# Last mixture of experts: blocks of 64 slots taken two at a time, activations as the stationary operand, a ring of eight weight buffers

## The chip, the cores and the metric

The kernel runs on one core of one Trainium2 chip. The metric is the device time of one launch in microseconds. The engines that matter here are TensorE (PE in the rows, with PEld for its weight loads), VectorE (DVE), ScalarE (ACT), GpSimd (POOL) and SyncE (SP), which issues the transfers. The kernel writes semaphores and waits by hand; nothing reorders its instructions.

## What is computed

Two layers run over 512 tokens of width 256, each of them attention, a second attention or memory part, and a feed-forward part. The change touches only the last part, the feed-forward part of the second layer: a mixture of eight experts in which each token goes to one.

```python
gate_scores = softmax(einsum('btd,de->bte', x, Wg) + bg)
top1_idx = argmax(gate_scores); top1_weight = gate_scores[top1_idx]
h = silu(einsum('btd,edh->bteh', x, W1) + b1)      # 256 -> 1024, 8 experts
o = einsum('bteh,ehd->bted', h, W2) + b2           # 1024 -> 256
y = sum(o * top1_mask) * top1_weight
x = x + y
```

## The kernel before

`program` runs `xattn0`, `memory0`, `ffn0`, `xattn1` and then `attn1_ffn1`, in which the class `Routed` is the last mixture. `Routed.prepare_sync` (L1985) and `prepare_gpsimd` run inside the attention layer `attn1`, so their loads and constants go beside that layer's work; `Routed.run` (L2016) is a block of its own, which all engines enter together.

P is 128, TT = 4 token tiles, DC = 2 halves of the width, E = 8 experts, NF = 8 pieces of the hidden width F = 1024. The tokens are sorted into blocks of 128 slots, each with one expert. Which expert has how many tokens is known only at run time, so the program always has NB = E + EXTRA = 8 + 3 = 11 blocks: block k below 8 is expert k's first block, and each of the three extra ones belongs to the expert that has overflowed, or to none. The number of an extra block's expert is computed by DVE (`expert`, semaphore `expert_ready`), read by SP into a register (`value_load`), and used in the address of its transfers.

For each block PE does three things, and for each two blocks a fourth:
- `gather(g)` (L2229): 16 products in fp32r with a 0/1 matrix `perm` that pick the tokens of two blocks into `gather_bank`, which DVE copies to `xg` (L2157);
- `hidden(k)` (L2243): 16 fp32 products, a 128x128 piece of `w1` stationary, the block's 128 columns of `xg` moving; the hidden values come out transposed, the hidden index on the partitions. ACT reads them from PSUM, adds the bias `b1` (one value for each partition) and applies Silu in one instruction, eight to a block (L2104), into `h`;
- `output(k)` (L2255): 8 fp32 products, a 128x128 piece of `h` stationary, 256 columns of `w2` moving, into `y_bank`. ACT casts the result to the high part `y_hi` (L2110), DVE forms the rest `y_lo` (L2188);
- `scatter(k)` (L2264): 8 products in fp32r of `permT` (made by DVE, L2162) with the two parts, added up in the banks 5 and 6.

The order on PE is hidden(k), for even k gather(k/2+1), output(k-1), scatter(k-2). The weights of a block are `w1` and `w2`, 1 MB each. Six pairs of buffers form a ring (RING = 6). `prepare_sync` fills all six; SP refills a buffer once `hidden` (for `w1`) or `output` (for `w2`) of the block that used it is done (`reload`, L2056). An fp32 product shows as two matmul records in the trace; an fp32r or bf16 product and a transpose show as one.

Of the kernel before, what the change touches and what calls it, by code (L numbers as in the profile page):

```python
# [19 lines left out]
E = 8  # L20
# [1920 lines left out]
class Routed:  # L1941
# [3 lines left out]
    RING = 6  # L1945

    def __init__(self, core, ctx, tag, weights, norm, out_d):
# [4 lines left out]
        self.EXTRA = (NT - 1) // P  # L1952
        self.NB = E + self.EXTRA
        self.NG = (self.NB + 1) // 2
        sb = lambda name, shape, dt=F32: core.sb(tag + name, shape, dt, ctx)
        self.w1 = [sb(f"_w1_{i}", [P, DC, self.F]) for i in range(self.RING)]
        self.w2 = [sb(f"_w2_{i}", [P, self.NF, D]) for i in range(self.RING)]
        self.b1, self.b2 = sb("_b1", [P, E, self.NF]), sb("_b2", [E, D])
        self.b1x = sb("_b1x", [P, self.EXTRA, self.NF])
        self.rw, self.rb = sb("_gate_w", [P, DC, E]), sb("_gate_b", [P, E])  # L1960
        self.slots = sb("_slots", [P, 2 * P * self.NG])
        self.rows = sb("_rows", [P, self.NB])
# [8 lines left out]
        self.w2_in = [sem(f"w2_{i}_in") for i in range(self.RING)]  # L1971

# [11 lines left out]

    def prepare_sync(self, sp):  # L1985
        sp.dma_start(self.rw[:], self.rw_d.rearrange("(c p) e -> p c e", p=P)).then_inc(self.gate_in, 16)
        sp.dma_start(self.rb[:], self.rb_d.partition_broadcast(P)).then_inc(self.gate_in, 16)
        sp.dma_start(self.b1[:], self.b1_d.rearrange("p (e f) -> p e f", e=E)).then_inc(self.b_in, 16)
        sp.dma_start(self.b2[:], self.b2_d).then_inc(self.b_in, 16)
        for k in range(self.RING):  # L1990
            self.load_w1(sp, k, k)
            self.load_w2(sp, k, k)
# [3 lines left out]
    def prepare_gpsimd(self, pool):  # L1996
# [5 lines left out]
        g.iota(self.rows[:], [[P, self.NB]], base=0, channel_multiplier=1, **exact).then_inc(self.const, 1)  # L2002
        g.iota(self.order[:], [[1, E]], base=-E, channel_multiplier=0, **exact).then_inc(self.const, 1)
        g.iota(self.first[:], [[-P, E]], base=(E - 1) * P, channel_multiplier=0, **exact).then_inc(self.const, 1)
        g.iota(self.steps[:], [[P, self.EXTRA]], base=P, channel_multiplier=0, **exact).then_inc(self.const, 1)
# [10 lines left out]
    def run(self):  # L2016
        core, nc, norm, tag = self.c, self.c.nc, self.norm, self.tag
        x, xn, xnT = core.x, core.xn, core.xnT
        NB, NG, NF, RING, EXTRA = self.NB, self.NG, self.NF, self.RING, self.EXTRA
        with ExitStack() as ctx:  # L2020
            sb = lambda name, shape, dt=F32: core.sb(tag + name, shape, dt, ctx)
            sem = lambda name: core.sem(tag + "_" + name)
            xs = [sb("_x_" + n, [P, TT, D], F32R) for n in ("hi", "lo")]
# [15 lines left out]
            h = [sb(f"_h{i}", [P, NF, P]) for i in range(2)]  # L2039
# [8 lines left out]
            g_psum, xg_ready, h_psum, h_ready = sem("g_psum"), sem("xg_ready"), sem("h_psum"), sem("h_ready")  # L2048
            y_psum, y_hi, y_lo, placed, b1x_in = (sem("y_psum"), sem("y_hi"), sem("y_lo"), sem("placed"),
                                                  sem("b1x_in"))  # L2050
            x_out, stored = sem("x_out"), sem("stored")
            gather_bank, y_bank, route_bank = core.bank(0), core.bank(1), core.bank(7)
            h_bank = lambda n: core.bank(2 + n % 3)
# [4 lines left out]
            def _(sp):  # L2058
                def reload(k, e):
                    sp.wait_ge(h_psum, 2 * (k - RING + 1))  # L2060
                    self.load_w1(sp, k, e)
                    sp.wait_ge(y_psum, k - RING + 1)
                    self.load_w2(sp, k, e)

                for k in range(RING, E):
                    reload(k, k)
                sp.wait_ge(expert_ready, 1)
                chosen = [sp.value_load(expert[0:1, i:i + 1], min_val=0, max_val=E - 1) for i in range(EXTRA)]
                for i in range(EXTRA):
                    sp.dma_start(self.b1x[:, i:i + 1, :],  # L2070
                                 self.b1_d.rearrange("p (e f) -> p e f", e=E)[:, bass.ds(chosen[i], 1), :]
                                 ).then_inc(b1x_in, 16)
                for i in range(EXTRA):
                    reload(E + i, chosen[i])
# [7 lines left out]
            def _(act):  # L2082
# [10 lines left out]
                act.wait_ge(self.b_in, 32)  # L2093
                for k in range(NB + 1):
                    if k < NB:
                        if k == E:
                            act.wait_ge(b1x_in, 16 * EXTRA)
                        if k >= 2:
                            act.wait_ge(y_psum, k - 1)
                        for f in range(NF):  # L2100
                            if f % 4 == 0:
                                act.wait_ge(h_psum, 2 * k + f // 4 + 1)
                            bias = self.b1[:, k, f:f + 1] if k < E else self.b1x[:, k - E, f:f + 1]
                            A.activation(h[k % 2][:, f, :], h_bank(2 * k + f // 4)[:, P * (f % 4):P * (f % 4) + P],  # L2104
                                         ACT.Silu, bias=bias).then_inc(h_ready, 1)
                    if k >= 1:
                        act.wait_ge(y_psum, k)
                        if k >= 3:
                            act.wait_ge(placed, k - 2)
                        A.copy(y[(k - 1) % 2][0][:], y_bank[:, 0:D]).then_inc(y_hi, 1)  # L2110

            @block.vector
            def _(dve):
# [23 lines left out]
                step(V.scalar_tensor_tensor(jump[:], first_x[:], float(P), self.first[:], ALU.mult, ALU.add))  # L2137
# [213 lines left out]
```

## Time and profile before

| what | us |
|---|---|
| device time, median of 3 runs (1106.3 to 1108.91) | 1106.91 |
| the profiled execution, its own time | 1106.76 |
| its span, first to last instruction | 1105.1 |
| TensorE busy in the span | 1005.0 (91%) |
| VectorE, ScalarE, GpSimd busy | 571.0, 498.9, 179.2 |
| start of the last mixture (its warm-up products) | at 979.27 |
| first product of the first hidden(0) | at 1001.70 |
| start of the final scatter's last record | at 1100.49 |

The profile's times are counted from the start of the span. The profiled execution took 1.66 us more than its span; this is what lies around the span. A record's duration holds a part at its end that the next one overlaps, so the pace of PE is read from the distance of starts, not from the mean duration. A group "128*64" has a stationary operand of 128 rows and 64 columns. In a DMA row the engine column says which engine's queue issued it.

### The profile page before, as it was taken

The page shows a single profiled execution, that of the slowest core. Times are in us where ns is not written, and L with a number is a line of the kernel's source. Part 1 is how long each engine was busy: PE and PEld are TensorE (multiplying, and loading weights), DVE is VectorE, ACT ScalarE, POOL GpSimd, SP SyncE. Part 2 cuts the span into 40 slices and gives each one's busy share as a digit, 9 for nine tenths or more (in the row PEclk, how much of TensorE's full clock was granted, in tenths as well). Part 3 has the DMA queues.
Part 4 walks back from the last instruction along what each step waited for, and adds up shares of the span by engine and source line. Part 5 has one row for each costly group of instructions (what it writes and reads, how often), then busy time and mean ns, then how long its engine had stood idle before and what let it go on. Part 6 is the DMA issues. An engine that isn't in the chain of part 4 may idle for free. (4 is left out here: it accounts for less than half of the span.)

```text
span 1105.1 us, 21134 instructions
## 1 busy us (share of the span) xinstructions
PE 1005.0 (91%) x8866; PEld 858.5 (78%) x8866; DVE 571.0 (52%) x811; ACT 498.9 (45%) x744; POOL 179.2 (16%) x164
## 2 busy tenths in 40 slices
PE   8899999727789999899999999999999998959998
PEld 6788888425469985588989898989898865559997
DVE  4577776495734345665545555454646412572211
ACT  5677776322346645535444444444544313213322
POOL 2000000203414423103030312111111004110000
PEclk9999999868779999999999999999999999879999
DMA  5111200102013204111111102020300005903610
GB/s 168 32 62 46 63 24 3 44 0 62 1 55 90 94 28 153 39 39 39 39 41 36 60 16 76 0 76 2 126 24 1 1 1 162 377 11 115 230 39 20
DMA packets 49396, 68.82 MB, mean 62 GB/s; under 512 B 5792, under 2 KB 40816, under 8 KB 49328
## 3 DMA queue, kind: packets, MB, share of 16 engines
q1 hardware_dynamic: 49328, 67.83, 18.7%
q8 instruction: 53, 0.87, 0.3%
q14 instruction: 15, 0.12, 0.0%
HBM read 67.29 MB, written 0.52 MB: 61 GB/s over the span
## 5 line engine op out<-in xcount | busy, mean ns | idle before, releaser
L1380 ACT ACTIVATE e_pr<-ps,e_negmax 128x1024 f32<-128x1024 f32 x64 | 71.4, 1115 | 171.0 <-DVE e_negmax L1385 164.8
L181 PE MATMUL ps<-f_pT_hi,f_cN_hi 128*128 128x256 f32 x512 | 146.1, 285 | 2.4 <-DVE f_pT_lo L1626 2.4
L181 PE MATMUL ps<-f_pT_hi,f_cN_lo 128*128 128x256 f32 x512 | 145.5, 284 | 0.0
L181 PE MATMUL ps<-f_pT_lo,f_cN_hi 128*128 128x256 f32 x512 | 145.4, 284 | 0.0
L1626 DVE TENSOR_TENSOR f_pT_lo<-ps,f_pT_hi 128x1024 fp32r<-128x1024 f32 x64 | 78.2, 1222 | 78.0 <-ACT f_pT_hi L1581 78.0
L181 PE MATMUL ps<-e_cT_hi,e_qb_hi 128*128 128x512 f32 x256 | 105.5, 412 | 0.0
L404 DVE SCALAR_TENSOR_TENSOR a_u<-ps,a_floor,a_cap 128x1024 f32<-128x1024 f32 x64 | 79.2, 1279 | 45.9 <-PE ps L485 45.9
L181 PEld LDWEIGHTS ps<-f_pT_hi,f_cN_hi 128*128 128x128 f32 x512 | 98.5, 192 | 4.6 <-DVE f_pT_lo L1626 2.6
L181 PE MATMUL ps<-e_cT_hi,e_qb_lo 128*128 128x512 f32 x256 | 100.6, 393 | 0.0
L181 PE MATMUL ps<-e_cT_lo,e_qb_hi 128*128 128x512 f32 x256 | 99.9, 390 | 0.0
L181 PEld LDWEIGHTS ps<-f_pT_lo,f_cN_hi 128*128 128x128 f32 x512 | 98.6, 193 | 1.5
L181 PEld LDWEIGHTS ps<-f_pT_hi,f_cN_lo 128*128 128x128 f32 x512 | 98.6, 193 | 0.0
L1385 DVE TENSOR_REDUCE e_negmax<-ps 128x1 f32<-128x1024 f32 x64 | 78.1, 1220 | 30.9 <-PE ps L181 30.2
L336 ACT ACTIVATE a_pr<-a_u,a_nb 128x1024 f32<-128x1024 f32 x64 | 73.8, 1154 | 44.4 <-DVE a_u L404 43.3
L1581 ACT CAST f_pT_hi<-ps 128x1024 fp32r<-128x1024 f32 x64 | 64.8, 1013 | 53.5 <-PE ps L1654 53.5
L1654 PE MATMUL ps<-ident,e_pr 128*128 128x128 f32 x512 | 66.5, 273 | 13.5 <-DVE f_pT_lo L1626 12.3
L100 PE MATMUL ps<-ident 128*128 128x128 f32 x240 | 40.9, 349 | 35.7 <-ACT b_cs L667 19.7
L1375 POOL TENSOR_TENSOR e_cT_lo<-e_rawT,e_cT_hi 128x512 fp32r<-128x512 f32 x32 | 40.4, 1295 | 193.6 <-ACT e_cT_hi L1563 193.6
L1654 PEld LDWEIGHTS ps<-ident,e_pr 128*128 128x128 f32 x512 | 57.0, 140 | 18.5 <-issue 18.3
L100 PEld LDWEIGHTS ps<-ident 128*128 128x128 f32 x240 | 39.4, 261 | 38.7 <-ACT b_cs L667 20.6
L1549 POOL TENSOR_TENSOR f_cN_lo<-e_raw,f_cN_hi 128x512 fp32r<-128x512 f32 x32 | 43.7, 1398 | 138.5 <-ACT f_cN_hi L1570 138.5
L181 PEld LDWEIGHTS ps<-e_cT_hi,e_qb_lo 128*128 128x128 f32 x256 | 48.0, 188 | 11.1
(360 smaller groups left out, 2137.1 us busy)
## 6 DMA issues: line engine op xcount, KB each, us to landing
k_w<-in_L_ffn_W SPq DMA_DIRECT2D x22, 1024.0 KB, 10.1
a_ctxT<-in_ctxT SPq DMA_DIRECT2D x16, 512.0 KB, 3.7
d_w<-in_L_ffn_w SPq DMA_DIRECT2D x32, 256.0 KB, 2.7
e_rawT<-in_ctxT SPq DMA_DIRECT2D x8, 1024.0 KB, 5.0
e_raw<-in_ctx SPq DMA_DIRECT2D x8, 1024.0 KB, 5.6
e_wq<-in_L_xattn_w_q SPq DMA_DIRECT2D x1, 1024.0 KB, 6.2
e_wk<-in_L_xattn_w_k SPq DMA_DIRECT2D x1, 1024.0 KB, 8.7
g_wv<-in_L_xattn_w_v SPq DMA_DIRECT2D x1, 1024.0 KB, 7.8
```

The source lines that it names most:

```text
L100: self.nc.tensor.matmul(self.bank(bank)[:, 0:P], self.ident[:], self.ident[:], start=True, stop=True)
L181: last = nc.tensor.matmul(out, a[i], b[j], start=start and n == 0, stop=stop and n == 2, skip_group_check=skip)
L336: A.activation(pr[:, n % NP, :], u[:, n % NU, :], ACT.Square, bias=nb[:], scale=HD ** -0.5).then_inc(p_ready, 1)
L404: V.scalar_tensor_tensor(u[:, n % NU, :].rearrange("p (r w) -> p r w", r=RT), core.psum[:, 0:2048].rearrange("p (r w) -> p r w", r=RT)[:, ...
L1375: nc.gpsimd.tensor_tensor(cT[1][:, c, cols], rawT[:, c, cols], cT[0][:, c, cols].bitcast(F32), ALU.subtract).then_inc(t_lo, 1)
L1380: nc.scalar.activation(pr[:, p % NPR, :], core.ps[p % 2][:], ACT.Exp, bias=negmax[:, p:p + 1], accum_out=total[:, p:p + 1]).then_inc(exp_r ...
L1385: nc.vector.tensor_reduce(negmax[:, p:p + 1], core.ps[p % 2][:], AX, ALU.max, negate=True).then_inc(max_ready, 1)
L1549: nc.gpsimd.tensor_tensor(cN[1][:, ks, :], raw[:, ks, :], cN[0][:, ks, :].bitcast(F32), ALU.subtract).then_inc(n_lo, 1)
L1581: nc.scalar.copy(pT[0][:, g, :, P * (p % 2):P * (p % 2) + P], core.ps[2][:].rearrange("p (k n) -> p k n", n=P)).then_inc(pT_hi, 1)
L1626: nc.vector.tensor_tensor(pT[1][:, g, :, cols], core.ps[2][:].rearrange("p (k n) -> p k n", n=P), pT[0][:, g, :, cols].bitcast(F32), ALU.s ...
L1654: last = nc.tensor.transpose(core.ps[2][:, k * P:(k + 1) * P], pr[:, p % NPR, k * P:(k + 1) * P], core.ident[:])
```

## The change

`Routed` alone is rewritten, and `layout` no longer transposes `L1_ffn_b1`.

- A block has BS = 64 slots. EXTRA becomes 511 // 64 = 7, NB = 15 blocks, NP = 8 pairs of blocks (the last pair has one block), NG = 4 gathers of 256 slots each in place of 6.
- `hidden(n)` works on a pair and on half of the hidden width, n = 0 to 15 (NCH). The 64 columns of `xg` of one block are the stationary operand and 512 columns of its `w1` the moving one. The first block's result goes to PSUM partitions 0 to 63, the second's to 64 to 127, and the two blocks' products alternate in the program.
- Hidden values now have the slot on the partitions, so the bias lies along the free axis. `b1` is loaded broadcast over 64 partitions for each block (256 KB written) and added by DVE (`biased`, new); ACT applies Silu in place on 128x512 (two to a pair), PE turns the result over with four transposes (`turn`, new), and ACT copies it from PSUM (`turned`, new).
- `output(n)` takes 64 columns of the turned `hT` of each block as the stationary operand and 256 columns of its own `w2` as the moving one; again the two blocks alternate on the two halves of the partitions.
- `scatter` and `y_hi`, `y_lo` work on a pair at a time.
- The ring has eight weight buffers. Six are filled by `prepare_sync` during `attn1` together with four of the bias loads; b2, the bias of blocks 4 to 7 and the weights of blocks 6 and 7 are issued by SP when `run` begins. The seven later blocks are loaded by pairs: `w1` when `hidden` of the pair four earlier is done, `b1` after its `biased`, `w2` after its `output`.

```diff
-    RING = 6
+    RING = 8
+    EARLY = 6
+    BS = 64
...
-        self.EXTRA = (NT - 1) // P
+        self.EXTRA = (NT - 1) // self.BS
...
+    def load_b1(self, sp, k, e):
+        one = slice(e, e + 1) if isinstance(e, int) else bass.ds(e, 1)
+        p, first = k // 2, self.BS * (k % 2)
+        i = p % (self.RING // 2)
+        sp.dma_start(self.b1[i][first:first + self.BS, :],
+                     self.b1_d[one, :].rearrange("o f -> (o f)").partition_broadcast(self.BS)
+                     ).then_inc(self.b1_in[i], 16)
...
-        for k in range(self.RING):
+        for k in range(self.EARLY):
             self.load_w1(sp, k, k)
+            if k < self.EARLY - 2:
+                self.load_b1(sp, k, k)
             self.load_w2(sp, k, k)
...
+                sp.dma_start(self.b2[:], self.b2_d).then_inc(self.b_in, 16)
+                for k in range(self.EARLY - 2, RING):
+                    if k >= self.EARLY:
+                        self.load_w1(sp, k, k)
+                    self.load_b1(sp, k, k)
+                    if k >= self.EARLY:
+                        self.load_w2(sp, k, k)
...
+                for n in range(NCH + 3):
+                    if n >= 4 and n % 2 == 0:
+                        high((n - 4) // 2)
+                    if 1 <= n <= NCH:
+                        turned(n - 1)
+                    if n < NCH:
+                        act.wait_ge(h_biased, n + 1)
+                        rows = rows_of(n // 2)
+                        A.activation(h[n % 2][0:rows, :], h[n % 2][0:rows, :], ACT.Silu).then_inc(h_ready, 1)
...
+                def biased(n):
+                    p, i = n // 2, n % 2
+                    dve.wait_ge(h_psum, n + 1)
+                    if i == 0:
+                        dve.wait_ge(self.b1_in[p % RP], 32 * (p // RP) + 16 * len(self.blocks(p)))
+                    if n >= 2:
+                        dve.wait_ge(hT_psum, n - 1)
+                    rows = rows_of(p)
+                    V.tensor_tensor(h[n % 2][0:rows, :], h_bank(n)[0:rows, :],
+                                    self.b1[p % RP][0:rows, 4 * P * i:4 * P * i + 4 * P], ALU.add
+                                    ).then_inc(h_biased, 1)
...
+                    for c in range(DC):
+                        for k in self.blocks(p):
+                            first, at = P * (p % 2) + BS * (k % 2), BS * (k % 2)
+                            last = t.matmul(h_bank(n)[at:at + BS, :], xg[(p // 2) % 2][:, c, first:first + BS],
+                                            self.w1[k % RING][:, c, 4 * P * i:4 * P * i + 4 * P], start=c == 0,
+                                            stop=c == DC - 1)
+                    last.then_inc(h_psum, 1)
...
+                    for f in range(4):
+                        last = t.transpose(hT_bank(n)[:, rows * f:rows * f + rows], h[n % 2][0:rows, f * P:(f + 1) * P],
+                                           core.ident[0:rows, 0:rows])
+                    last.then_inc(hT_psum, 1)
...
+                    for f in range(4):
+                        for k in self.blocks(p):
+                            at = BS * (k % 2)
+                            last = t.matmul(y_bank[at:at + BS, 0:D], hT[n % 2][:, f, at:at + BS],
+                                            self.w2[k % RING][:, 4 * i + f, :], start=i == 0 and f == 0,
+                                            stop=i == 1 and f == 3)
                     last.then_inc(y_psum, 1)
...
-                for k in range(NB + 2):
-                    if k < NB:
-                        hidden(k)
-                    if k % 2 == 0 and k // 2 + 1 < NG:
-                        gather(k // 2 + 1)
-                    if 1 <= k <= NB:
-                        output(k - 1)
-                    if k >= 2:
-                        scatter(k - 2)
+                for n in range(NCH + 3):
+                    if n < NCH:
+                        hidden(n)
+                    if 1 <= n <= NCH:
+                        turn(n - 1)
+                    if 2 <= n <= NCH + 1:
+                        output(n - 2)
+                    if n % 4 == 1 and n // 4 + 1 < NG:
+                        gather(n // 4 + 1)
+                    if n >= 4 and n % 2 == 0:
+                        scatter((n - 4) // 2)
```

How PE's program reads in the middle of the mixture. In the kernel before, one block without a gather (k_xg and k_h are activations, k_w_3 the first weights of block 3, k_w_2 the second weights of block 2):

```order
L2243 MATMUL ps<-k_xg,k_w_3 128x128 x16
L2255 MATMUL ps<-k_w_2,k_h 128x256 x8
```

In the changed kernel, one half of the pair of blocks 4 and 5 with the second half of the pair 2 and 3 behind it:

```order
L2302 MATMUL ps<-k_w_4,k_xg 64x512 [waits k_h_biased]
L2302 MATMUL ps<-k_w_5,k_xg 64x512
L2302 MATMUL ps<-k_w_4,k_xg 64x512
L2302 MATMUL ps<-k_w_5,k_xg 64x512
L2315 MATMUL ps<-ident,k_h 128x128 [waits k_hT_ready,k_h_ready]
L2315 MATMUL ps<-ident,k_h 128x128 x3
L2330 MATMUL ps<-k_w_2,k_hT 64x256 [waits k_hT_ready]
L2330 MATMUL ps<-k_w_3,k_hT 64x256
L2330 MATMUL ps<-k_w_2,k_hT 64x256
L2330 MATMUL ps<-k_w_3,k_hT 64x256
```

The stationary and the moving operand of `hidden` have changed places, four transposes stand between `hidden` and `output`, and each of the products writes 64 rows where it wrote 128.

SP's program after `run` begins. Before, it starts with reloads (which wait for blocks 0 and 1), then reads three expert numbers:

```order
L1976 DMA k_w_0<-in_L_ffn_W 128x2x1024
L1982 DMA k_w_0<-in_L_ffn_W 128x8x256
L1976 DMA k_w_1<-in_L_ffn_W 128x2x1024
L1982 DMA k_w_1<-in_L_ffn_W 128x8x256
L2068 TENSOR_LOAD k_expert
L2068 ISA x2
```

In the changed kernel it starts with transfers that wait for nothing, then reads seven expert numbers, of which the first two lines stand here:

```order
L2095 DMA k_b<-in_L_ffn_b 8x256
L1992 DMA k_b_2<-in_L_ffn_b 64x1024 x2
L1979 DMA k_w_6<-in_L_ffn_W 128x2x1024
L1992 DMA k_b_3<-in_L_ffn_b 64x1024
L1985 DMA k_w_6<-in_L_ffn_W 128x8x256
L1979 DMA k_w_7<-in_L_ffn_W 128x2x1024
L1992 DMA k_b_3<-in_L_ffn_b 64x1024
L1985 DMA k_w_7<-in_L_ffn_W 128x8x256
L2103 TENSOR_LOAD k_expert [waits c_pT_psum]
L2103 ISA x2
```

Every later load now stands behind the reading of the seven numbers (the name in the brackets of that line is that of a semaphore released earlier and used again; it is the wait for `expert_ready`), and the loads of a pair stand in the order w1, w1, b1, b1, w2, w2, so the next pair's w1 stands behind the wait of this pair's w2.

## Rows read from the trace of the kernel before

**Rows 1.** Windows (core us; each engine busy and count; clock, DMA share, GB/s)
```profile
979.00:1001.70 22.70, 20.05 (x131) 18.92 (x131) 13.51 (x56) 4.41 (x7) 0.00 (x0) 0.71 0.00 1
1001.70:1100.80 99.10, 98.00 (x697) 92.90 (x696) 16.51 (x44) 30.35 (x100) 0.00 (x0) 1.00 0.31 107
```
**Rows 2.** Timeline, PE, two blocks: start, us, engine, line, out<-in, shape, count
```profile
1024.17 3.73 PE L2243 MATMUL ps<-k_xg,k_w 128*128 128x128 f32 x32
1027.74 3.62 PE L2255 MATMUL ps<-k_w,k_h 128*128 128x256 f32 x16
1031.01 0.47 PE L2264 MATMUL ps<-k_y_hi,k_permT 128*128 128x256 f32 x1
1032.15 3.73 PE L2243 MATMUL ps<-k_xg,k_w 128*128 128x128 f32 x32
1035.64 0.37 PE L2229 MATMUL ps<-k_perm,k_x_hi 128*128 128x256 f32 x1
1037.63 3.62 PE L2255 MATMUL ps<-k_w,k_h 128*128 128x256 f32 x16
```
**Rows 3.** Timeline, the last block: the wait for y_lo and the final scatter
```profile
1094.87 3.69 PE L2255 MATMUL ps<-k_w,k_h 128*128 128x256 f32 x16 [1.00 <-DVE k_y_lo L2188]
1099.58 0.36 PE L2264 MATMUL ps<-k_y_hi,k_permT 128*128 128x256 f32 x1
```
**Rows 4.** Source view of lines with 64 stationary columns: ns min/median/max, first and last start
```profile
L1724 PE MATMUL ps<-e_qc,g_wv x64: 592/592/645, 891.0 to 904.4; 128*64 128x512 f32 x64
L734 PE MATMUL ps<-xnT,b_wdt x4: 593/593/643, 209.1 to 210.4; 128*64 128x512 f32 x4
```
**Rows 5.** Timeline, PE, first layer: shapes of 128, 32-row, 32-column and 128 in turn
```profile
101.70 0.39 PE L181 MATMUL ps<-a_ctx_hi,a_wkv_lo 128*128 128x512 f32 x1
102.02 1.17 PE L485 MATMUL ps<-a_qd,a_kT 32*128 32x128 f32 x32
103.12 1.10 PE L505 MATMUL ps<-a_pr,a_v 128*32 128x64 f32 x64
104.15 0.50 PE L181 MATMUL ps<-a_ctx_hi,a_wkv_hi 128*128 128x512 f32 x1
104.49 0.40 PE L181 MATMUL ps<-a_ctx_lo,a_wkv_hi 128*128 128x512 f32 x1
```
**Rows 6.** Timeline, PE, `xattn1`: eight transposes and the record behind them
```profile
872.51 1.03 PE L1654 MATMUL ps<-ident,e_pr 128*128 128x128 f32 x8
873.30 0.36 PE L181 MATMUL ps<-f_pT_hi,f_cN_hi 128*128 128x256 f32 x1
```
**Rows 7.** Timeline, ACT and DVE operations of 128x512 and 128x256
```profile
936.62 2.54 ACT L1841 ACTIVATE h_sig<-h_q,h_aug 128x512 f32<-128x512 f32 x4
985.94 0.58 ACT L163 COPY xnT<-ps 128x512 f32<-128x512 f32 x1 [4.42 <-PE ps L171]
1003.83 1.28 ACT L2104 ACT_TABLE_LOAD   x1 [3.37 <-PE ps L2243]
1014.49 0.37 ACT L2110 CAST k_y_hi<-ps 128x256 fp32r<-128x256 f32 x1 [2.31 <-PE ps L2255]
1014.90 0.42 DVE L2188 TENSOR_TENSOR k_y_lo<-ps,k_y_hi 128x256 fp32r<-128x256 f32 x1 [5.30 <-ACT k_y_hi L2110]
998.99 0.69 DVE L2157 COPY k_xg<-ps 128x512 f32<-128x512 f32 x1 [3.95 <-PE ps L2229]
```
**Rows 8.** Windows again: the early weight loads, and one with late loads
```profile
940.00:946.00 6.00, 6.00 (x15) 2.66 (x14) 1.72 (x3) 0.69 (x1) 0.00 (x0) 1.00 1.07 379
964.00:970.00 6.00, 4.62 (x19) 3.35 (x18) 3.95 (x5) 0.00 (x0) 3.13 (x3) 0.94 0.66 225
1034.00:1038.00 4.00, 4.00 (x35) 3.97 (x35) 0.00 (x0) 2.28 (x8) 0.00 (x0) 1.00 1.07 395
```
**Rows 9.** SP's timeline around the three expert numbers, and DVE's row that makes them
```profile
1023.42 0.37 SPq L1982 DMA_DIRECT2D k_w<-in_L_ffn_W  x1
1025.90 1.43 SPq L2070 DMA_DIRECT2D k_b1x<-in_L_ffn_b  x3
...
1001.07 0.17 DVE L2173 TENSOR_SCALAR k_expert<-k_owner 128x3 int32<-128x3 f32 x1
```

More of the change, by code:

```diff
@@ L1971, in __init__ @@
         self.w2_in = [sem(f"w2_{i}_in") for i in range(self.RING)]
+        self.b1_in = [sem(f"b1_{i}_in") for i in range(self.RING // 2)]
     def load_w1(self, sp, k, e):
@@ L2022, in run @@
             sem = lambda name: core.sem(tag + "_" + name)
+            late = range(self.EARLY, RING)
+            self.w1 += [sb(f"_w1_{i}", [P, DC, self.F]) for i in late]
+            self.w2 += [sb(f"_w2_{i}", [P, NF, D]) for i in late]
+            self.b1 += [sb(f"_b1_{i}", [P, self.F]) for i in range(len(self.b1), RP)]
+            self.b2 = sb("_b2", [E, D])
             xs = [sb("_x_" + n, [P, TT, D], F32R) for n in ("hi", "lo")]
@@ L2249, in output, with hidden @@
-                def output(k):
-                    pe.wait_ge(self.w2_in[k % RING], 16 * (k // RING) + 16)
-                    pe.wait_ge(h_ready, NF * (k + 1))
-                    if k >= 1:
-                        pe.wait_ge(y_lo, k)
-                    for f in range(NF):
-                        last = t.matmul(y_bank[:, 0:D], h[k % 2][:, f, :], self.w2[k % RING][:, f, :], start=f == 0,
-                                        stop=f == NF - 1)
+                def hidden(n):
+                    p, i = n // 2, n % 2
+                    if i == 0:
+                        pe.wait_ge(xg_ready, p // 2 + 1)
+                        for k in self.blocks(p):
+                            pe.wait_ge(self.w1_in[k % RING], 16 * (k // RING) + 16)
+                    if n >= 2:
+                        pe.wait_ge(h_biased, n - 1)
+                    for c in range(DC):
[5 more added lines that the diff above has]
+                    last.then_inc(h_psum, 1)
@@ new lines, in output @@
+                def output(n):
+                    p, i = n // 2, n % 2
+                    pe.wait_ge(hT_ready, n + 1)
+                    if i == 0:
+                        for k in self.blocks(p):
+                            pe.wait_ge(self.w2_in[k % RING], 16 * (k // RING) + 16)
+                        if p >= 1:
+                            pe.wait_ge(y_lo, p)
+                    for f in range(4):
+                        for k in self.blocks(p):
+                            at = BS * (k % 2)
+                            last = t.matmul(y_bank[at:at + BS, 0:D], hT[n % 2][:, f, at:at + BS],
+                                            self.w2[k % RING][:, 4 * i + f, :], start=i == 0 and f == 0,
+                                            stop=i == 1 and f == 3)
@@ L2274, in _ @@
                 pe.wait_ge(mineT_ready, 1)
-                pe.wait_ge(self.b_in, 32)
+                pe.wait_ge(self.b_in, 16)
                 for j in range(TT):
```

158 lines of the change are left out of this document (78 added, 80 removed).

## The prediction

> **What bounds the kernel now.** I read the windows first. From the first `hidden` to the last scatter, 99.10 us, TensorE is busy 98.00 us at a granted clock of 1.00, which is the 2.4 GHz level, while DVE has 16.51 us of work and ACT 30.35 [rows 1]. So in this stretch PE alone sets the time; the waits of DVE and ACT cost nothing. The stretch before it, 979.0 to 1001.7, is routing (logits, ranks, first gather), and the change leaves its chain alone. What counts is the price of one block on PE, and there I take distances of starts in the timeline [rows 2]: hidden 1027.74 - 1024.17 = 3.57 us, output 1031.01 - 1027.74 = 3.27, scatter 1032.15 - 1031.01 = 1.14, gather 1037.63 - 1035.64 = 1.99. Eleven blocks at 7.98 are 87.8 us, five gathers in the loop 9.9, together 97.7. The other 1.4 us of the 99.1 is mostly the 1.00 us wait for y_lo ahead of the last output and the short gap before the final scatter [rows 3].
>
> **The two big terms: hidden and output.** They hang on whether two products with 64 stationary columns, one into each half of the partitions, run side by side. The trace has both cases [rows 4]. L734 writes one half only: four records of 512 columns start 209.1 to 210.4, so 1.3 / 3 = 0.43 us each. L1724 writes both halves with different moving data: 64 records of the same shape from 891.0 to 904.4, 13.4 / 63 = 0.213 us each. The same shape costs half where both halves are used, so the pairing is real for fp32.
> - Hidden: 8 records a step (2 blocks x 2 halves of the width x 2 records) at 0.213 = 1.71 us. The last pair has one block: 4 records at 0.43 = 1.72. Sixteen steps: 27.3 us.
> - Output: 16 records a step with 256 columns, half of 0.213, so 16 x 0.107 = 1.71 us; the lone block again the same. Sixteen steps: 27.3 us. L1724 sends the two halves in groups, this code alternates them record pair by record pair; the 32-column products of L505 alternate over four parts, 64 records in 104.15 - 103.12 = 1.03 us [rows 5], 0.016 each, though 64 columns at the 512-column pace of L734 would take 0.43 / 8 = 0.054. Alternation does not break the overlap.
>
> **Turns, scatters, gathers.** Eight transposes take 873.30 - 872.51 = 0.79 us [rows 6], 0.099 each; 64 of them are 6.3 us, all new and all on PE. Eight scatters at 1.14 are 9.1, three gathers in the loop at 1.99 are 6.0. Sum of PE's work: 27.3 + 27.3 + 6.3 + 9.1 + 6.0 = 76.0 us, against 97.7.
>
> **Changing shape.** PE now goes from 64 columns to 128 (turn) and back in every step. In the first layer [rows 5] the record ahead of L485 starts at 101.70 and has 0.23 us of pace, L485 starts at 102.02: 0.09 lost. L505 to L181: the first record takes 104.49 - 104.15 = 0.34 in place of 0.23: 0.11 lost. The kernel has 48 steps of hidden, turn and output; I put 0.12 us on each, 5.8 us. The bounds are 0 (hidden follows output in the same shape, and a part of the change is already in the scatter's 1.14) and 0.3, which is a record emptied wholly: record duration 0.40 less its pace 0.23 gives 0.17 [rows 5], and about as much again for a weight load that was ahead before and is not now. 48 x 0.18 = 8.6 us more at the one bound, 5.8 less at the other.
> The Trainium skill has a rule that speaks against this change, in TensorEngine Tiling (Array Packing), Key Properties: changing the tiling mode drains the engine. The rows agree that something is lost, 0.09 and 0.11 us, and the page gives no price; by a full drain the sum would be that of the 0.3 bound.
>
> **Waits between the engines.** A step's result goes hidden, DVE bias, ACT Silu, PE turn, ACT copy, PE output. Bias: a 128x512 DVE copy out of PSUM takes 0.69 us; Silu: four 128x512 ACT operations took 2.54, so 0.64; copy 0.58; y_hi 0.37 and y_lo 0.42 as now [rows 7]. Between hidden(n) and turn(n) PE has turn(n-1), output(n-2) and hidden(n+1), 4 us, for 0.69 + 0.64 and some 0.3 of signalling; between turn(n) and output(n) again about 4 us for 0.58. DVE has per pair 2 x 0.69 + 0.42 + maps, ACT 2 x (0.64 + 0.58) + 0.37 = 2.8 us out of some 10. So these are hidden in the middle. They are not at the ends. At the start turn(0) has only hidden(1) ahead of it (1.71 + 0.12) and needs 0.69 + the Silu table's 1.28 + 0.64 + 0.3 = 2.9: 1.1 us of waiting. At the end the last output waits 0.6 us for y_lo and the last scatter 1.1 for its own y: 1.7, where the old loop lost 1.4.
> Sum from the first hidden to the last scatter: 76.0 + 5.8 + 1.1 + 1.7 = 84.6 us against 99.1. That is 14.5 us less.
>
> **Weights.** 15 blocks need 31.5 MB and 3.9 MB of broadcast bias, where 11 needed 23.1. A pair (4.7 MB with its bias) at 379 GB/s [rows 8] takes 12.4 us, longer than the 10.6 us PE takes for one, so only the head start of the ring hides it.
> - Early: the six buffers now have 1.05 MB of bias among them, 2.8 us more. The old loads end inside 964 to 970 [rows 8], the block ends at 979: hidden. Then 5.2 MB go at 979, 13.8 us, landed by about 995; first used at about 1018 (bias of blocks 4, 5) and 1029 (block 6). SP has issued them before it needs `expert`, made at 1001.07 [rows 9]. No cost, and DVE and ACT are not seen slower: PE kept full pace at 379 GB/s (6.00 of 6.00 busy).
> - The seven numbers: three took from 1023.79 to 1025.90, 2.1 us [rows 9]; seven take 4.9, so SP is free at 1006.2, while hidden(1), which it must await anyway, ends at about 1005.3. No cost.
> - Late: w1 of pair p+1 stands behind the wait of w2 of pair p, that is behind output of the pair four earlier. Walking this through at 385 GB/s, w1 for blocks 12 and 13 lands at about 1044 and is wanted at 1059; for block 14 at 1053, wanted at 1069. Slack 15 us, so no cost. A late window shows 395 GB/s beside a PE busy 4.00 of 4.00 [rows 8].
>
> The profiled execution took 1106.76 (the median is 1106.91, the same within 0.3%, which is about what a measurement of this kernel can tell from no change). 1106.76 - 14.5 = 1092.3; I say **1092.5**.
>
> **Rivals.**
> - *Each change of shape empties PE* (0.2 to 0.3 us on each step): 1096.5 to 1101. For it: 0.5 of duration on the first L181 record. Against: 0.09 and 0.11 in the distances [rows 5]. Chance 0.13, taken at 1099.
> - *Changes of shape are nearly free*, or outputs are as cheap as now (3.27 for 3.41): 1085 to 1088. Chance 0.07.
> - *The pairs overlap only in part.* 54.6 us of hidden and output, 7/8 of it paired, is 47.8; at 0.27 us in place of 0.213, 12.7 us come back: 1105. Chance 0.06, since 64 records of L1724 stand against it. The Trainium skill, in TensorE: Matmul & The Clock Gate (Measured speedup vs the span model), gives 2.38 for three column parts, 0.79 of the ideal; L1724 shows 2.0 for two, and the measurement decides.
> - *The pairs do not overlap at all*: the 47.8 us are paid twice, 1092.3 + 47.8 = 1140. It decides from 0.277 us a record, where 14.5 / 47.8 = 30% is gone. Chance 0.04. **Slower.**
> - *The weights come late.* The weights of block 12 come late below about 240 GB/s while the queue is full, for instance through the broadcasts, which read one 4 KB row 64 times. At 200 GB/s hidden(12) waits 7 us and hidden(14) 9: 1109. **Slower.** For it: 4.7 MB a pair is more than the pace. Against: 379 and 395 GB/s [rows 8]. Chance 0.07.
> - *The chain of DVE and ACT sets the pace*: it must take over 4 us in place of 1.6 a leg. 1098. Chance 0.03.
>
> **How the numbers follow.** The forecast has 0.60, with 1089 to 1097 as its own range. Faster by over 0.3% means below 1103.4: 0.60 + 0.13 + 0.07 + 0.03, and 0.02 of the partial overlap, 0.85. Slower, above 1110.1: no overlap and most of late weights, 0.09. Between: 0.06. The range 1087 to 1102 takes in the dear changes of shape and most of the cheap ones; outside are partial and no overlap, late weights and a little below.
>
> **What would show it.** Records of the new hidden line 0.21 us apart and of output 0.107; the last scatter ending near 1086 in the trace, a loop of about 85 us; turn about 0.4 us; PE's waits in the loop under 4 us, none of them for a DMA; clock 1.00; starts of hidden to turn to output showing 0.1 us beyond the pace. If records of hidden lie 0.27 or more apart the first step is wrong; if PE waits for k_w the weights' step is.

## The result, and the profile after

The changed kernel takes 1094.31 us (median of 4 runs, 1091.08 to 1096.21), the kernel before 1107.91 in the same session (4 runs, 1106.3 to 1109.89). The ratio is 0.9881, its 95% interval 0.9852 to 0.991: 13.6 us less, where the forecast was 1092.5 us, 14.4 less than the median of before as it stood then (1106.91). Ratios are formed from launches at like clock: one of the four launches of a later experiment (both blocks into the same half) took 1508.48 us at a mean granted clock of 0.64 and is left out of its ratio. The profiled execution of the changed kernel took 1096.21 us, 1.7 of it outside its span.

First the windows of the changed kernel (columns as in [rows 1]): the routing ahead of the first `hidden`, the loop from the first `hidden` to just before the end of the last scatter, and the end of the early weight loads.

```profile
984.40:1005.20 20.80, 18.28 (x130) 17.22 (x130) 13.58 (x55) 5.59 (x8) 0.00 (x0) 0.83 0.90 250
1005.23:1090.10 84.87, 83.24 (x537) 45.53 (x536) 21.85 (x45) 20.62 (x41) 0.00 (x0) 1.00 0.64 196
976.00:982.00 6.00, 0.72 (x4) 0.30 (x2) 5.43 (x21) 0.20 (x1) 1.27 (x7) 0.95 0.86 302
```

The last record of the final scatter starts at 1089.94 and ends at 1090.22. So the loop, from the first `hidden` to that end, takes 85.0 us where it took 99.1 [rows 1]; PE is busy for 83.24 us of the window shown, and the clock is at its upper level throughout, as before. The timeline of PE in the middle (start, duration, line, operands, count) answers to [rows 2]:

```profile
1015.53 1.89 PE L2302 MATMUL ps<-k_w,k_xg 128*64 128x512 f32 x8
1017.35 0.66 PE L2315 MATMUL ps<-ident,k_h 128*128 128x128 f32 x4
1017.94 1.95 PE L2330 MATMUL ps<-k_w,k_hT 128*64 128x256 f32 x16
1019.71 1.89 PE L2302 MATMUL ps<-k_w,k_xg 128*64 128x512 f32 x8
1021.53 0.65 PE L2315 MATMUL ps<-ident,k_h 128*128 128x128 f32 x4
1022.12 1.95 PE L2330 MATMUL ps<-k_w,k_hT 128*64 128x256 f32 x16
1023.99 0.39 PE L2341 MATMUL ps<-k_y_hi,k_permT 128*128 128x256 f32 x1
```

From start to start, `hidden` (L2302) is 1.82 us, `turn` (L2315) 0.59, `output` (L2330) 1.77, together 4.18; in front of a scatter (L2341) or a gather an output is 1.87, and a hidden behind one as well. The last two waits of PE, the only ones in the loop, and what ACT does at the start and DVE in the loop (a group: count, then busy us and mean ns of one):

```profile
1083.11 1.91 PE L2330 MATMUL ps<-k_w,k_hT 128*64 128x256 f32 x8 [0.63 <-DVE k_y_lo L2235]
1089.04 0.35 PE L2341 MATMUL ps<-k_y_hi,k_permT 64*128 64x256 f32 x1 [1.00 <-DVE k_y_lo L2235]
```

```profile
1004.02 1.28 ACT L2148 ACT_TABLE_LOAD   x1
1007.94 0.63 ACT L2148 ACTIVATE k_h<-k_h 128x512 f32<-128x512 f32 x1 [2.64 <-DVE k_h L2228]
```

```profile
L2228 DVE TENSOR_TENSOR k_h<-ps,k_b 128x512 f32<-128x512 f32 (+1 forms) x16 | 11.1, 691 | 38.0 <-PE ps L2302 38.0
L2148 ACT ACTIVATE k_h<-k_h 128x512 f32<-128x512 f32 (+1 forms) x16 | 10.1, 633 | 2.6 <-DVE k_h L2228 2.6
L2130 ACT COPY k_hT<-ps 128x512 f32<-128x512 f32 (+1 forms) x16 | 8.9, 559 | 49.2 <-PE ps L2315 49.2
```

**Where the difference of the two traces comes from.** The loop gives back 14.1 us, but the spans differ by 10.6 only (1105.1 and 1094.5). The other terms: the mixture starts at 984.54 instead of 979.27, 5.3 later, and the routing takes 20.7 us in place of 22.4, 1.7 less; its granted clock is 0.83 in the first window above, against 0.71 before [rows 1]. The later start is seen in the warm-up products at the start of the mixture, first of before, then of after:

```profile
979.27 5.46 PE L100 MATMUL ps<-ident 128*128 128x128 f32 x24 [7.82 <-PEq L1750]
```

```profile
984.54 4.66 PE L100 MATMUL ps<-ident 128*128 128x128 f32 x24 [7.82 <-PEq L1750]
```

The later start has grown up in layers whose code is the same: L734 starts at 212.6 in place of 209.1 [rows 4], L1724 at 896.3 in place of 891.0. In their windows the granted clock is lower, 0.90 against 0.97 in the first 50 us; of after, then of before:

```profile
0.00:50.00 50.00, 40.89 (x481) 33.99 (x482) 23.50 (x36) 25.94 (x35) 6.37 (x16) 0.90 0.34 100
```

```profile
0.00:50.00 50.00, 41.64 (x520) 34.88 (x524) 25.06 (x37) 28.44 (x39) 6.37 (x16) 0.97 0.32 100
```

The attention layer that shares its time with the new loads takes 50.5 us in both traces.

### The profile page after: what moved, and what is told of

Same layout as the page of the kernel before. It is cut to its first block and busy times, and to the rows that moved or that the text cites. A ratio compares the mean times of both kernels' runs of the same rounds, so it can differ in the third digit from the quotient of the medians.

```text
span 1094.5 us, 20836 instructions
## 1 busy us (share of the span) xinstructions
PE 993.8 (91%) x8706; PEld 814.5 (74%) x8706; DVE 576.6 (53%) x811; ACT 490.5 (45%) x685; POOL 178.7 (16%) x164
## 5 line engine op out<-in xcount | busy, mean ns | idle before, releaser
L100 PE MATMUL ps<-ident 128*128 128x128 f32 x240 | 39.5, 341 | 35.6 <-ACT b_cs L667 19.7
```

Source lines behind the costliest of these rows:

```text
L100: self.nc.tensor.matmul(self.bank(bank)[:, 0:P], self.ident[:], self.ident[:], start=True, stop=True)
```

## The experiments

All are edits of the changed kernel. The ratio is always to the kernel before on the same chip, whose median was 1108.75 us beside the changed kernel again, the same half, one block's products first and the ring of six; 1108.22 beside the groups of two, the pairs, the split last block and the 64 different rows; 1108.38 beside the last two. It is worked out launch against launch, so it need not be the quotient of the two medians. "Loop" is the time from the first `hidden` to the end of the last scatter, 85.0 us in the changed kernel.

### The changed kernel again

The first question was whether the 5.3 us belong to the change (its early loads beside the attention layer) or to the chip. The kernel is not edited.

> The changed kernel once more, unedited. In the first pair of traces the loop from first hidden to last scatter is 84.9 us where it was 99.1, but the last mixture starts 5.3 us later (984.5 against 979.3) behind layers whose code is the same, with a lower granted clock in the first 50 us (0.90 against 0.97) and between 400 and 450 (0.90 against 0.97). Theory A: that late start is the clock's and comes and goes from run to run; then the start of the mixture differs in this trace by 1 us or more from 984.5 and the loop is again 84.9 within 0.3. Theory B: the longer weight loads (bias broadcasts among them) slow the attention layer; then that layer, from its first h_wq product to the end of its block, takes longer than in the kernel before (50.7 us from 927.2 to 977.9) by more than 1 us in both traces of the changed kernel.

1092.99 us (1092.62 to 1098.01), ratio 0.9877 (0.9841 to 0.9913). The mixture starts at 981.34, the loop takes 85.0 us, the attention layer 50.5. In the twelve traces of this study the start goes with the granted clock of the 880 us ahead, whatever was edited: 983.9 to 984.5 in the five where the window from 0 to 880 us has 0.95, 979.3 to 981.3 in the seven where it has 0.96. The kernel with the split last block below has all the early loads of the changed kernel and starts at 979.35, within 0.1 us of before. The later start comes with the lower clock in the layers ahead, not from the change; why the clock differs from run to run stays open.

### Both blocks into the same half

Does the gain come from the two halves of the partitions working side by side?

```diff
-  first, at = P * (p % 2) + BS * (k % 2), BS * (k % 2)
-  t.matmul(h_bank(n)[at:at + BS, :], ...)
+  first = P * (p % 2) + BS * (k % 2)
+  t.matmul(h_bank(n)[0:BS, :], ...)       # both blocks; output likewise into y_bank[0:BS]
```

> Both blocks of a pair write PSUM partitions 0 to 63 (one accumulation group over both), so no two products can use different column halves; the number, shapes and order of all instructions stay. Leaves out: the second block's own result, the two are added up. Theory A (the whole gain of the pairing is the two column halves working side by side): hidden and output records go from 0.213 and 0.107 us apart to 0.427 and 0.213, 7/8 of 54.6 us is paid again, 47.8 us more than the changed kernel, about 1142. Rival (a product with 64 stationary columns is cheap by itself): no change, 1094.

1141.27 us (median of three launches, 1140.74 to 1145.31), ratio 1.0317 (1.0275 to 1.0359). The loop takes 133.0 us, 48.1 more. Its timeline of PE:

```profile
1014.78 0.66 PE L2316 MATMUL ps<-ident,k_h 128*128 128x128 f32 x4
1015.36 3.67 PE L2331 MATMUL ps<-k_w,k_hT 128*64 128x256 f32 x16
1018.87 3.60 PE L2302 MATMUL ps<-k_w,k_xg 128*64 128x512 f32 x8
1022.39 0.66 PE L2316 MATMUL ps<-ident,k_h 128*128 128x128 f32 x4
```

`hidden` is 3.52 us instead of 1.82, `output` 3.51 instead of 1.77. The same products with the same data from the same buffers cost twice as much when they write one half. The forecast's own figure for this, 47.8 us, was right to 0.3.

### One block's products, then the other's

Does it matter that the two blocks alternate?

```diff
-  for c in range(DC):
-      for k in self.blocks(p):
+  for k in self.blocks(p):
+      for c in range(DC):
   ...
-  for f in range(4):
-      for k in self.blocks(p):
+  for k in self.blocks(p):
+      for f in range(4):
```

> Within a step all products of the first block come first and then all of the second, where they alternated. Theory A (each half has its own queue deep enough, as L1724 shows with groups of four records): no change, within 0.3% of the changed kernel, records 0.213 apart. Rival (records start strictly in order, so two halves overlap only where they alternate): a hidden step is 4 + 4 records of which only one pair overlaps, 7 x 0.427 = 3.0 in place of 1.71 us, an output step 15 x 0.213 = 3.2 in place of 1.71: 14 x 2.8 = 39 us more.

1106.72 us (1103.08 to 1109.92), ratio 0.9987 (0.997 to 1.0004): the gain is gone, and neither theory said so. The loop takes 97.1 us, 12.1 more. Its timeline shows which step pays:

```profile
1027.31 1.94 PE L2302 MATMUL ps<-k_w,k_xg 128*64 128x512 f32 x8
1029.19 0.66 PE L2315 MATMUL ps<-ident,k_h 128*128 128x128 f32 x4
1029.77 2.86 PE L2330 MATMUL ps<-k_w,k_hT 128*64 128x256 f32 x16
1032.56 0.39 PE L2286 MATMUL ps<-k_perm,k_x_hi 128*128 128x256 f32 x1
```

`hidden`, whose groups are four records long (two products of two records), still takes 1.88 us. `output`, whose groups are eight, takes 2.79 in place of 1.87, 0.92 more. Thirteen such steps make 12.0 of the 12.1; the fourteenth costs 0.1, because the lone last block's `hidden`, which needs the first half only, runs beside its second group. So two halves overlap fully only if the other half's record comes soon enough in the program. Where a `hidden` follows an `output` directly, the rows show the look ahead itself:

```profile
1013.19 2.21 PE L2330 MATMUL ps<-k_w,k_hT 128*64 128x256 f32 x13
1015.03 0.64 PE L2302 MATMUL ps<-k_w,k_xg 128*64 128x512 f32 x1
1015.24 0.59 PE L2330 MATMUL ps<-k_w,k_hT 128*64 128x256 f32 x2
1015.51 0.59 PE L2302 MATMUL ps<-k_w,k_xg 128*64 128x512 f32 x1
1015.67 0.38 PE L2330 MATMUL ps<-k_w,k_hT 128*64 128x256 f32 x1
1015.89 1.88 PE L2302 MATMUL ps<-k_w,k_xg 128*64 128x512 f32 x6
```

In the program all 16 records of the output stand ahead of `hidden`. In time, a first record of `hidden`, which writes the first half, starts before the last three records of the output, which write the second, and another before the last one. An estimate from these rows: the second group's eight records, at 0.213 us each, end by 1015.89, so they began near 1014.19, 1.0 us or four to five records behind the first group.

### The output in groups of two products

If some four records are what PE looks past, groups of two products (four records) must cost nothing.

```diff
-  for f in range(4):
-      for k in self.blocks(p):
+  for f, k in [(2 * a + b, k) for a in range(2) for k in self.blocks(p) for b in range(2)]:
```

> Output steps in groups of two products (four records) for a block, then two for the other, and so on. In e2_grouped the hidden steps, with groups of four records, cost the same as alternating (1.88 us), and the output steps, with groups of eight records, 2.79 us in place of 1.77. Theory E (PE looks only about four records ahead for one that the other half can take): groups of four cost nothing, 1.77 us a step, the time of the changed kernel. Rival F (it is the time in a row on one half that counts, or each change of the half costs): output steps lie between 1.77 and 2.79 us, about 0.5 us dearer, 7 us in all.

1093.46 us (1093.11 to 1094.68), ratio 0.9871 (0.9856 to 0.9887). The outputs sum up to 30.0 us where they made 29.5, the loop is 85.7, 0.7 more. Four records cost next to nothing, eight cost 0.92 us a step. Lengths between were not tried.

### The steps of a pair together

How much do the changes of shape cost? The two `hidden` of a pair, its two `output` and its two `turn` are put side by side, so that there are half as many changes; ACT and DVE follow the same order.

```diff
-  for n in range(NCH + 3):
-      if n < NCH:
-          hidden(n)
-      if 1 <= n <= NCH:
-          turn(n - 1)
-      if 2 <= n <= NCH + 1:
-          output(n - 2)
+  for p in range(NP + 3):
+      if p < NP:
+          hidden(2 * p); hidden(2 * p + 1)
+      if 2 <= p < NP + 2:
+          output(2 * p - 4); output(2 * p - 3)
+      if 1 <= p <= NP:
+          turn(2 * p - 2); turn(2 * p - 1)
```

> The same work in another order: both halves' hidden of pair p, then both outputs of pair p-2 (all with 64 stationary columns), then both turns of pair p-1, the gather and scatter(p-3) (all with 128). Two changes of shape a pair in place of four or more. Theory A (0.35 us is lost in each of the 16 cycles hidden, turn, output, as the traces of the changed kernel show: 1.82 + 0.59 + 1.77 against 1.71 + 0.41 + 1.71): half of it is saved, 2.8 us, and the waits of 0.6 and 1.0 us for y_lo at the end go, since other work stands there: 4 us less than the changed kernel, a loop of about 81 us. Rival (the extra is the price of a first record behind a wait or of the transposes themselves, not of the change of shape): only the 1 to 1.5 us of the end are saved.

1089.55 us (1088.3 to 1090.2), ratio 0.9833 (0.982 to 0.9847). The loop takes 80.6 us, 4.4 less. Its timeline of PE:

```profile
1022.54 3.65 PE L2305 MATMUL ps<-k_w,k_xg 128*64 128x512 f32 x16
1026.02 3.62 PE L2333 MATMUL ps<-k_w,k_hT 128*64 128x256 f32 x32
1029.58 1.09 PE L2318 MATMUL ps<-ident,k_h 128*128 128x128 f32 x8
1030.42 0.36 PE L2344 MATMUL ps<-k_y_hi,k_permT 128*128 128x256 f32 x1
```

Two hidden, two outputs and two turns take 3.48 + 3.56 + 0.84 = 7.88 us, where two cycles of the changed kernel take 8.36. The eight transposes in a row are back at 0.84, near the 0.79 of [rows 6]; four alone had cost 0.59. The second `hidden` of a pair waits for a semaphore of its own as before and yet costs no more than its pace, so it is the change of shape that costs and not the first record behind a wait.

Over the whole loop `hidden`, `output` and `turn` take 63.4 us in place of 67.9, some 4.5 less. The two waits for y_lo at the end are gone, but two others have come: 0.54 us for DVE near the start, and this one ahead of the last block:

```profile
1061.99 3.19 PE L2305 MATMUL ps<-k_w,k_xg 128*64 128x512 f32 x7 [1.42 <-issue]
```

The profile names no releaser for it, but in the trace the first weights of block 14 land at 1061.90, 0.09 us before this record. With PE faster, the weights have begun to be late.

### The last block over both halves

The last pair has one block, whose products fill one half only. Here its two halves of the hidden width go side by side, its two partial outputs too, and the last scatter adds them.

```diff
+  steps = lambda p: [n for n in (2 * p, 2 * p + 1) if n < NCH]     # the last pair has one step
-      for k in self.blocks(p):
+      for side in range(2):
+          k, part = (2 * p, side) if p == LAST else (2 * p + side, i)
```

> As e4_by_pair, and the lone last block uses both column halves: each half takes one half of the hidden width, and the scatter adds the two partial outputs up. Theory A (a lone block takes 1.71 us a step like a pair, because one column half is idle): one hidden step, one output step and 0.4 us of transposes are saved, 3.8 us more than e4_by_pair saves, a loop of about 77 us, 7 to 8 us less than the changed kernel. Rival: weights become the limit as PE gets faster (15 us a pair of transfers with broadcasts against 9 on PE), and PE waits for k_w before pair 6 or 7; then less than 5 us are saved.

1084.64 us (1083.66 to 1088.52), ratio 0.9798 (0.9783 to 0.9813), the fastest of all; the loop takes 75.9 us, 4.8 less again. Its window, and its last output and scatters in the timeline:

```profile
1001.80:1078.00 76.20, 74.94 (x533) 46.34 (x532) 20.91 (x45) 19.25 (x39) 0.00 (x0) 1.00 0.68 218
```

```profile
1073.50 1.95 PE L2346 MATMUL ps<-k_w,k_hT 128*64 128x256 f32 x16
1075.38 0.38 PE L2357 MATMUL ps<-k_y_hi,k_permT 128*128 128x256 f32 x1
...
1076.47 0.36 PE L2357 MATMUL ps<-k_y_hi,k_permT 128*128 128x256 f32 x1
```

One hidden and one output less save 3.4 us at the pace of 1.71 each, one turn 0.2. Another 1.0 comes from the wait ahead of the last block, 1.42 before and 0.38 here:

```profile
1061.07 1.94 PE L2317 MATMUL ps<-k_w,k_xg 128*64 128x512 f32 x8 [0.38 <-issue]
```

Its weights land at 1060.98, again 0.09 us ahead of the record. So the rival that the weights become the limit has come true in a small part: PE does wait for them, for 0.38 us.

### A ring of six buffers

Are the two more buffers needed, and what slows the loads?

```diff
-    RING = 8
+    RING = 6
...
+                for p in range(RP, E // 2):
+                    reload(p, self.blocks(p))
                 sp.wait_ge(expert_ready, 1)
```

> Six weight buffers in place of eight: blocks 6 and 7 are reloaded after the first pair, everything later one pair later. Theory A, at the full rate of 385 GB/s: no wait for weights, within 1 us of the changed kernel. Theory C (the trace of the changed kernel shows the broadcasts of the bias to be slow: with the DMA engines busy throughout, 319 GB/s from 1025 to 1065 and dips to about 200; I put 2.2 us on each 256 KB broadcast): by a walk through the queues hidden(12) waits 2.5 us and hidden(14) 3.1 us for weights, 5.6 us more than the changed kernel.

1101.03 us (1097.88 to 1104.85), ratio 0.9938 (0.9916 to 0.9959), the loop 90.3 us, 5.3 more than with eight. PE's timeline, and two windows behind the wait:

```profile
1064.54 2.72 PE L2304 MATMUL ps<-k_w,k_xg 128*64 128x512 f32 x8 [3.24 <-DMA k_w<-in_L_ffn_W]
1067.18 1.12 PE L2317 MATMUL ps<-ident,k_h 128*128 128x128 f32 x4
1068.23 2.29 PE L2332 MATMUL ps<-k_w,k_hT 128*64 128x256 f32 x16
```

```profile
1064.00:1067.00 3.00, 2.46 (x8) 0.57 (x8) 0.00 (x0) 0.00 (x0) 0.00 (x0) 0.76 1.09 302
1067.00:1070.00 3.00, 3.00 (x20) 1.88 (x20) 0.69 (x1) 1.11 (x2) 0.00 (x0) 0.67 1.10 366
```

The size of the loss came out near what theory C had, 5.6, but by coincidence: its second wait, 3.1 us at hidden(14), did not come. The loss is made of two other parts: one wait of 3.24 us for the weights of block 12, and a granted clock that falls behind the wait. It is 0.76 and 0.67 in these two windows, which lie partly at 2.4 GHz and partly at 1.2. The three steps there take 2.64, 1.05 and 2.22 us instead of 1.87, 0.59 and 1.77: another 1.7. Two windows of 4 us of this kernel show what holds the loads up, the first with first weights in the queue, the second with the bias of two blocks:

```profile
1041.00:1045.00 4.00, 4.00 (x33) 2.49 (x29) 0.69 (x1) 1.11 (x2) 0.00 (x0) 1.00 1.03 409
1045.00:1049.00 4.00, 4.00 (x27) 1.96 (x28) 0.69 (x1) 1.12 (x2) 0.00 (x0) 1.00 1.05 210
```

The queue is full in both (share 1.03 and 1.05), but it moves 409 GB/s in one and 210 in the other. The next three runs ask why; all have the ring of six.

### The bias read from 64 different rows

```diff
-  self.b1_d[one, :].rearrange("o f -> (o f)").partition_broadcast(self.BS)
+  self.w1_d[one, 0:self.BS, :].rearrange("o p f -> (o p) f")
```

> As e3_ring6, but each bias load reads 64 different rows of 4 KB (of w1) in place of one row 64 times; as many bytes and packets of the same size to the same place. Leaves out: the bias has other values. Theory C (reading one row 64 times is what is slow): no dips in the transfer rate (at least 375 GB/s with the DMA engines busy, where e3_ring6 has 325), hidden(12) does not wait for weights, and the loop is 84.9 us as with the ring of eight. Rival D (writing 64 partitions, or the 4 KB packets of small loads, is slow): unchanged, a wait of 3.2 us and a loop of 90.3.

1101.8 us (1099.29 to 1104.08), ratio 0.9948 (0.9929 to 0.9967), a loop of 89.5, with a wait of 2.35 us for the same weights. The window over the bias loads, 217 GB/s:

```profile
1047.00:1051.00 4.00, 4.00 (x30) 2.12 (x27) 0.69 (x1) 1.49 (x3) 0.00 (x0) 1.00 1.03 217
```

The rate over 1025 to 1055 us is 333 GB/s, as with the broadcast (332). That the broadcast reads one row 64 times is not the reason for the dips. The wait is 0.9 us shorter than forecast, which stays unexplained.

### The bias of a pair in one transfer to 128 partitions, and no late bias at all

```diff
-  p, first = k // 2, self.BS * (k % 2)
-  sp.dma_start(self.b1[i][first:first + self.BS, :], ...partition_broadcast(self.BS)
+  if k % 2 == 0:
+      sp.dma_start(self.b1[i][:], ...partition_broadcast(P)
```

> As e3_ring6, but the bias of a pair comes in one transfer that writes all 128 partitions (the first block's bias in both halves), where it came in two that write 64 each; 512 KB a pair as before, still one row read many times. Leaves out: the second block of a pair gets the first one's bias. e6_ring6_rows showed that reading one row many times is not what makes these transfers slow (about 225 GB/s in their dips, where those of w1 show 400 to 415 and of w2 350). Theory G (a transfer into half of the partitions runs at about half the rate): the dips go, the rate with busy DMA engines is 375 GB/s, the wait of hidden(12) is under 1.5 us. Rival H (some fixed cost of each small transfer): the dips are half as long, and hidden(12) waits about 2.5 us in place of 3.2.

1095.78 us (1090.47 to 1098.44), ratio 0.9872 (0.9836 to 0.9908). No wait for weights, the loop 85.0 us, and the same bytes of bias pass at 366 GB/s:

```profile
1047.00:1051.00 4.00, 4.00 (x26) 2.17 (x28) 0.69 (x1) 0.47 (x1) 0.00 (x0) 1.00 1.06 366
```

The last run leaves the late bias loads out:

```diff
-  for k, e in zip(self.blocks(p), experts):
-      self.load_b1(sp, k, e)
```

> As e3_ring6, with no bias loads for the pairs behind the ring. Leaves out: these pairs get an older pair's bias. It prices the late bias loads: 1.84 MB less until hidden(12) is due, at 225 GB/s some 6 us earlier. Theory G or H alike: hidden(12) does not wait, the loop is 84.9 us as with the ring of eight. Rival (the ring of six is short without them too, since w2 shows 350 GB/s and each load waits behind an earlier one's release): hidden(12) still waits over 1 us.

1096.15 us (1090.88 to 1097.83), ratio 0.9874 (0.9842 to 0.9906), loop 85.0, no wait for weights. Over 1025 to 1055 us the three kernels move 332 GB/s (bias to 64 partitions), 371 (to 128) and 368 (none). A fixed cost of each small transfer (rival H) would have left dips half as long, and there are none. The packets in the trace say the same: those of 4 KB last 0.16 us on average while first weights pass (from 1041 us in the ring of six) and also while the bias goes to 128 partitions (1047 to 1049), but 0.34 while it goes to 64 (1045.5 to 1048.5). What is slow is the transfer into half of the partitions. The Trainium skill has this in SBUF — State Buffer, section Door 1: The DMA port swizzle: partitions 0 to 63 reach 8 of 16 ports, 64 to 127 the other 8, and it states an asymptote of some 218 GB/s for 8 ports. The trace agrees: 210 and 217. The port itself is not seen in any row.

## Why the prediction was right

**What bounds the kernel** was read correctly: PE alone sets the loop, and the loop's difference is the kernel's. The sum, step by step (84.6 forecast, 85.0 measured):

| term | forecast | measured |
|---|---|---|
| `hidden`, 16 steps with their change of shape | 29.2 | 29.5 |
| `output`, likewise | 29.2 | 29.5 |
| `turn`, likewise | 8.2 | 8.9 |
| scatters | 9.1 | 9.2 |
| gathers in the loop | 6.0 | 6.3 |
| waits at start and end | 2.8 | 1.6 |

- *The halves work side by side.* Right, and shown: undone, the loop gets 48.1 us longer. The reasoning from L505 that alternation does no harm [rows 5] was right and too weak: alternation, or groups of no more than some four records, is needed. Groups of eight records, which the two source rows [rows 4] do not warn of, give back 12.1 of 14.1 us. I had no rival for that, since the code alternates.
- *Changes of shape.* Right in kind, somewhat low in size. In the middle, a cycle of 4.18 us against 1.71 + 0.41 + 1.71 = 3.83 leaves 0.35, 0.117 a step, where 0.12 was put down. But a step beside a scatter or gather costs 1.87, and in all the 48 steps take 67.9 us where their pace makes 60.9: 7.0, not 5.8, or 0.146 a step. That it is the changes was shown by making fewer of them: some 4.5 us less in these steps, for a gain of 4.4. The rule of the Trainium skill that I had set against the rows was TensorEngine Tiling (Array Packing), Key Properties: changing the mode drains the engine. A step costs 0.12 to 0.15 us here, not the 0.3 that I had put on a record emptied wholly.
- *The turn* was mis-sized by 0.7 us in sum: I took 0.099 us a transpose from eight in a row [rows 6], but four with a change on either side take 0.59. Eight take 0.84 in the run by pairs, so by these two a transpose takes some 0.06 and the change 0.34: the 0.099 already held a part of the change.
- *The wait of 1.1 us at turn(0)* was wrong. I had added the Silu table's 1.28 us, because before it stood behind the wait for PE [rows 7]. After, ACT loads it at 1004.02, right behind its previous copy and before `hidden(0)` has begun, and Silu starts at 1007.94. The wait that did not come, 1.1, makes up for hidden, output, turn and gathers, which took 1.6 more than forecast, so the sum's closeness is in part luck. Why the load comes ahead of the wait here was not tested.
- *The waits at the end* were 0.63 and 1.00, forecast 0.6 and 1.1. The bias, Silu and copy cost 0.69, 0.63 and 0.56 to 0.59, forecast 0.69, 0.64 and 0.58.
- *The weights* were right in their result, that PE waits for none, and wrong in their size. I gave all bytes 379 to 385 GB/s. Before, the early loads ended inside 964 to 970 [rows 8]; with the 2.8 us that I added, and the 5.3 by which this run is late, they should have ended by 978, but they still run in 976 to 982. The set issued when the mixture begins lasts some 20 us, not 13.8; between 1025 and 1065 the rate is 319 GB/s. The first weights of block 14, which I had landing 16 us before they are wanted, land 10 us before (1062.5 and 1072.5). The reason in the loop is the bias, whose transfers fill 64 partitions each and move at 210. It also explains more than half of the early loads' delay: from the first issue to the last landing they take 39.5 us before, 48.3 after, and 43.6 where the bias goes to 128 partitions; the rest was not taken apart. It was the fifth rival ("through the broadcasts"), with the right culprit and the wrong reason: not the repeated row. The eight buffers cover it; with six it costs 5.3 us, and in the two faster kernels, with eight, PE waits 1.42 and 0.38 us for block 14.

The forecast's sum for the profiled execution was 1092.3. It took 1096.21, since the layers ahead ran 5.3 us late and the routing was 1.7 us shorter; without the two it would be 1092.7. The kernel before varies too, from 1104.25 to 1111.77 in 19 runs, and the times of one pair of traces say less than the loops in them.

## What to carry to other kernels

With 64 stationary columns, put the second tile on the other half of the partitions and alternate the two product by product; eight fp32 records of one half in a row are too many. Group steps by the shape of their products, and fill the lone last tile by splitting its own work over both halves. Load what is broadcast to two half tiles in one transfer to all 128 partitions where the halves want the same data, or count it at half the rate.

## What the runs showed of the chip

- PE overlaps products of two column halves when groups are four records long (1.88 us for eight records of 512 columns), and no longer fully at eight (2.79 in place of 1.87 us for 16 of 256 columns); records of a later instruction for the free half start first. The rule of the Trainium skill in TensorE: Matmul & The Clock Gate (The mechanism) says that products start and end strictly in program order. The starts in this trace differ from it.
- A transfer into 64 partitions moves 210 to 217 GB/s with the queue full, the same bytes in one transfer to 128 partitions 366.
- A wait of 3.24 us of PE in the middle of dense work was followed by a granted clock of 0.76 and 0.67 and cost another 1.7 us. Behind the wait of 2.35 us (64 different rows) the same two windows have 0.86 and 0.57, and that loop loses 2.1 us beside the wait. Behind the wait of 1.42 us (steps of a pair together) the clock stays at 1.00. A wait in the middle of the loop can cost more than it lasts.
- The same code ahead of the mixture ended between 979.3 and 984.5 us in twelve traces, the late ends at a mean granted clock of 0.95 and the early ones at 0.96.
